# A four-layer attention and expert kernel: the shared expert's down products one step behind, its logits leaving per batch

## The reference

```python
logits = x @ w_router.T
_, top_idx = jax.lax.top_k(logits, TOP_K)
mask = jax.nn.one_hot(top_idx, E, dtype=logits.dtype).sum(axis=1)
scores = jax.nn.sigmoid(logits) * mask
...
shared = jax.nn.silu(x @ w_gate.T) * (x @ w_up.T) @ w_down.T
out = shared + expert_out.sum(axis=0)
...
x = x + _L0_xattn_ref(ctx_1024, _layernorm(x, axis=-1), ...)
x = x + _L0_ffn_ref(_layernorm(x, axis=-1), L0_ffn_w_router, ...)
x = x + _L1_xattn_ref(_layernorm(x, axis=-1), ctx_1024, ...)
x = x + _L1_ffn_ref(_layernorm(x, axis=-1), L1_ffn_gate_w, ...)
```

## Time and profile before

| what | value |
|---|---|
| time, median of 3 runs | 1640.59 us (1637.47 to 1646.26) |
| the profiled execution, its own time | 1626.23 us |
| its span, first to last instruction | 1624.5 us |
| PE busy | 1455.4 us (90%) |
| DVE, ACT, POOL busy | 942.9, 872.7, 638.1 us |
| mean granted clock of PE | 0.954 |

### The profile page before, as it was taken

One profiled execution on the slowest core, in us unless ns is written; L12 is line 12 of the kernel. 1 busy time (PEld: TensorE's weight loads), 2 busy tenths in 40 slices (PEclk: granted clock), 3 DMA queues, 4 the chain that ended last, 5 costly groups with the idle time before them and its releaser, 6 DMA issues. The chain is left out here.

```text
span 1624.5 us, 28386 instructions
## 1 busy us (share of the span) xinstructions
PE 1455.4 (90%) x9884; PEld 1191.8 (73%) x9884; DVE 942.9 (58%) x1771; ACT 872.7 (54%) x2184; POOL 638.1 (39%) x886
## 2 busy tenths in 40 slices
PE   4999999999999999888899994799998539999995
PEld 3878887878787888577888883566564528888885
DVE  5776767676767676655211116577787554444442
ACT  3886868677878686634111123566664214454442
POOL 6514444434444440322300015332321035777764
PEclk9999999999999999979999996999999559999998
DMA  4400000000000000012789853000000413455442
GB/s 135 167 1 21 1 21 2 21 3 20 2 20 2 1 2 1 1 34 72 267 310 316 306 192 48 26 8 14 8 1 1 136 52 116 118 127 119 119 124 27
DMA packets 74448, 120.27 MB, mean 74 GB/s; under 512 B 7008, under 2 KB 55136, under 8 KB 74304
## 3 DMA queue, kind: packets, MB, share of 16 engines
q1 hardware_dynamic: 63600, 101.76, 19.3%
q0 software_dynamic: 10704, 16.65, 5.1%
HBM read 99.78 MB, written 18.61 MB: 73 GB/s over the span
## 5 line engine op out<-in xcount | busy, mean ns | idle before, releaser
L508 ACT ACTIVATE a_p<-a_s,a_negmax 128x512 f32<-128x512 f32 x256 | 176.1, 688 | 111.4 <-DVE a_negmax L632 61.4
L632 DVE TENSOR_REDUCE a_negmax<-a_s 128x1 f32<-128x512 f32 x256 | 176.3, 689 | 74.3 <-PE a_s L371 68.0
L273 POOL TENSOR_TENSOR a_o_l<-a_o,a_o_h 128x256 fp32r<-128x256 f32 x64 | 46.9, 734 | 297.7 <-ACT a_o_h L533 297.7
L1546 ACT ACTIVATE h_probs<-h_scores,h_negmax 128x256 f32<-128x256 f32 x256 | 117.8, 473 | 82.0 <-DVE h_negmax L1713 82.0
L380 PEld LDWEIGHTS a_t<-ident,a_p 128*128 128x128 f32 x1024 | 122.3, 140 | 51.3 <-issue 22.8
L380 PE MATMUL a_t<-ident,a_p 128*128 128x128 f32 x1024 | 156.7, 276 | 0.7 <-DVE a_pT L647 0.7
L1958 POOL TENSOR_TENSOR n_w_l<-n_raw,n_w_h 128x768 fp32r<-128x768 f32 x64 | 118.1, 1847 | 74.6 <-ACT n_w_h L2001 74.6
L398 PE MATMUL a_out_p<-a_pT,a_v 128*64 128x256 f32 x1024 | 124.6, 385 | 0.0
L370 PE MATMUL a_s<-a_k_hl,a_q_hh 128*128 128x512 f32 x256 | 106.2, 415 | 2.2 <-issue 1.5
L1713 DVE TENSOR_REDUCE h_negmax<-h_scores 128x4 f32<-128x1024 f32 x64 | 78.0, 1219 | 49.5 <-PE h_scores L1640 49.5
L1651 PEld LDWEIGHTS h_turned<-ident,h_probs 128*128 128x128 f32 x512 | 55.1, 142 | 64.6 <-issue 45.8
(11 more groups left out here) (358 smaller groups left out, 4376.3 us busy)
## 6 DMA issues: line engine op xcount, KB each, us to landing
e_w_in<-in_L_ffn_gate_up_proj SPq DMA_DIRECT2D x31, 1024.0 KB, 7.1
n_raw<-in_L_ffn_w SPq DMA_DIRECT2D x64, 384.0 KB, 3.1
e_w_out<-in_L_ffn_down_proj SPq DMA_DIRECT2D x31, 512.0 KB, 5.3
rows_in<-a_zeros SPq DMA_DIRECT2D x1, 3968.0 KB, 15.8
e_rows<-rows_in SPq DMA_DIRECT2D x31, 128.0 KB, 5.1
rows_out<-e_result POOLq DMA_DIRECT2D x31, 128.0 KB, 4.8
a_both<-in_ctx SPq DMA_DIRECT2D x8, 256.0 KB, 2.8
a_both<-in_x SPq DMA_DIRECT2D x8, 256.0 KB, 3.0
```

Of the source, the lines that this page charges most:

```text
L508: act.activation(probs[j][:, :], scores[j % 2][:, :], ACT.Exp, bias=negmax[:, j:j + 1], accum_out=total[:, r % 2, j % 2, j // 2:j // 2 + 1 ...
L632: dve.tensor_reduce(negmax[:, j:j + 1], scores[j % 2][:, :], AX.X, ALU.max, negate=True).then_inc(max_set, 1)
L1546: ins = act.activation(probs[s % 4][:, j, :], scores[s % 2][:, j // 2, j % 2, :], ACT.Exp, bias=negmax[:, s % 4, j:j + 1], accum_out=total ...
```

## The change

What it does, with "unit" as above:

- `down` takes one chunk: `down(n)`, 12 matmuls, stands in PE's stream behind gate and up of unit n + 1. The four chunks of a group add up in PSUM, so the first of them waits for `add` of the group before (`added`). `s_hid_h` and `s_hid_l` are two buffers of one chunk each in place of one of four.
- The logits of a batch go to the bank of `small` that its transposes came through. DVE's new `take_logits(b)` sums their two halves into `r_logits` (64 elements in, 32 out, per partition). `turn_x(b)` now waits for `take_logits` of batch b - 2, not only for `xT_l`. In a unit, `find_logits(2n)` stands ahead of gate, and `find_logits(2n + 1)` between gate and up.
- route(0) stands inside unit 3 ahead of `s_hidden`, route(1) after unit 3, route(2) and route(3) after unit 4, route(4) after unit 5; `count` after unit 3 on PE. Two copies of route(0) go. `add(grp)` follows the units 4, 8 and the last early one.

```diff
-        hid_h, hid_l = sb("s_hid_h", [P, FC, N], F32R), sb("s_hid_l", [P, FC, N], F32R)
+        hid_h, hid_l = [sb(f"s_hid_h{i}", [P, N], F32R) for i in range(2)], [sb(f"s_hid_l{i}", [P, N], F32R) for i in range(2)]
...
-        logit_ps = sum_ps[1][:, :, :].rearrange("p i (t h e) -> p (i t) h e", h=2, e=E)
-        logits = within
+
+        logit_ps = [w[:, 0, 0:4 * E].rearrange("p (t h e) -> p t h e", h=2, e=E) for w in small]
+        logits = sb("r_logits", [P, NT, E])
...
-                def down(grp):
-                    pe.wait_ge(low, FC * (grp + 1))
-
-                    wait(pe, added, grp)
-                    passes = [(h, w, c) for c in range(FC)
-                              for h, w in ((hid_h, sw_h), (hid_h, sw_l), (hid_l, sw_h))]
+                def down(n):
+                    m, grp = n % FC, n // FC
+                    pe.wait_ge(low, n + 1)
+                    if m == 0:
+
+                        wait(pe, added, grp)
+                    if n == 0:
+                        pe.wait_ge(sl_set, 4)
                     for t in range(TILES):
-                        for k, (h, w, c) in enumerate(passes):
-                            ins = pe.matmul(sum_ps[t // 2][:, t % 2, :], h[:, c, t * P:(t + 1) * P], w[2][:, c, :],
-                                            start=(k == 0), stop=(k == len(passes) - 1))
-                    ins.then_inc(summed, 1)
+                        passes = ((hid_h, sw_h), (hid_h, sw_l), (hid_l, sw_h))
+                        for k, (h, w) in enumerate(passes):
+
+                            ins = pe.matmul(sum_ps[t // 2][:, t % 2, :], h[n % 2][:, t * P:(t + 1) * P], w[2][:, m, :],
+                                            start=(m == 0 and k == 0 and t % 2 == 0),
+                                            stop=(m == FC - 1 and k == len(passes) - 1 and t % 2 == 1))
+                    ins.then_inc(downed, 1)
...
-                    wait(pe, x_low, b - 1)
+                    wait(pe, logits_set, b - 1)
...
                 def find_logits(b):
                     pe.wait_ge(x_low, b + 1)
-                    for t in range(2 * b, 2 * b + 2):
-                        at = slice(t * P, (t + 1) * P)
+                    if b == 0:
+                        pe.wait_ge(rl_set, 1)
+                    for t in range(2):
+                        at = slice((2 * b + t) * P, (2 * b + t + 1) * P)
                         for kc in range(KC):
-                            pe.matmul(logit_ps[:, t, :, :], g.xT_h[:, kc, at], router_hl[:, kc, :, :], start=(kc == 0), stop=False)
-                            ins = pe.matmul(logit_ps[:, t, 0, :], g.xT_l[:, kc, at], router_hl[:, kc, 0, :], start=False, stop=(kc == KC - 1))
-                    if b == NB - 1:
-                        ins.then_inc(logits_done, 1)
+                            pe.matmul(logit_ps[b % 2][:, t, :, :], g.xT_h[:, kc, at], router_hl[:, kc, :, :], start=(kc == 0), stop=False)
+                            ins = pe.matmul(logit_ps[b % 2][:, t, 0, :], g.xT_l[:, kc, at], router_hl[:, kc, 0, :], start=False, stop=(kc == KC - 1))
+                    ins.then_inc(logits_done, 1)
 
                 def shared(n, first):
 
                     wait(pe, hidden_set, n - 1)
+                    if n < NB // 2:
+                        find_logits(2 * n)
                     if n % FC == 0 and n // FC * 2 < NB:
                         pe.wait_ge(x_low, 2 * (n // FC) + 2)
                     if n == 0:
                         pe.wait_ge(sl_set, 1)
                     product(gate_ps[n % 2], 0, n, gated)
                     if n < NB // 2:
-                        if n == 0:
-                            pe.wait_ge(rl_set, 1)
-                        find_logits(2 * n)
                         if 2 * n + 2 < NB:
                             turn_x(2 * n + 2)
+                        find_logits(2 * n + 1)
                     if n == 0:
                         pe.wait_ge(sl_set, 2)
                     product(up_ps[n % 2], 1, n, upped)
-                    if n < NB // 2:
-                        find_logits(2 * n + 1)
-                        if 2 * n + 3 < NB:
-                            turn_x(2 * n + 3)
-                    if n % FC == 0 and n > first:
-                        if n == FC:
-                            pe.wait_ge(sl_set, 4)
-
-                            pe.wait_ge(hot_set, 1)
-                        down(n // FC - 1)
+                    if 2 * n + 3 < NB:
+                        turn_x(2 * n + 3)
+                    if n > first:
+                        down(n - 1)
...
                     shared(n, 0)
-                    if n == FC:
+                    if n == FC - 1:
                         count()
-                down(EARLY - 1)
+                down(FC * EARLY - 1)
...
-                    down(GROUPS - 1)
+                    down(FC * GROUPS - 1)
...
-                    wait(act, summed, n // FC)
-                    act.activation(hid_h[:, n % FC, :], hidden[n % 2][:, :], ACT.Copy).then_inc(high, 1)
+                    wait(act, downed, n - 1)
+                    act.activation(hid_h[n % 2][:, :], hidden[n % 2][:, :], ACT.Copy).then_inc(high, 1)
...
-                        dve.wait_ge(logits_done, 1)
-                        link(dve.tensor_copy(logits[:, :, :], logit_ps[:, :, 1, :]))
-                        link(dve.tensor_tensor(logits[:, :, :], logit_ps[:, :, 0, :], logits[:, :, :], ALU.add))
+                        dve.wait_ge(logits_set, NB)
...
+                def take_logits(b):
+                    dve.wait_ge(logits_done, b + 1)
+                    dve.tensor_reduce(logits[:, 2 * b:2 * b + 2, :], logit_ps[b % 2].rearrange("p t h e -> p t e h"),
+                                      AX.X, ALU.add).then_inc(logits_set, 1)
...
                 def shared(n):
-                    if 2 * n + 2 < NB:
-                        take_low(2 * n + 2)
+                    if n < NB // 2:
+                        take_logits(2 * n)
+                        if 2 * n + 2 < NB:
+                            take_low(2 * n + 2)
+                        take_logits(2 * n + 1)
                         if 2 * n + 4 < NB:
                             apply(2 * n + 4)
+                    if n == NB // 2 - 1:
+                        route(0)
...
-                    dve.wait_ge(summed, grp + 1)
+                    dve.wait_ge(downed, FC * (grp + 1))
...
-                    if n in range(3, 8):
-                        route(n - 3)
+                    if n == 3:
+                        route(1)
+                    elif n == 4:
+                        route(2)
+                        route(3)
+                    elif n == 5:
+                        route(4)
                     elif n == 8:
                         scale_queries()
-                    if n % FC == 1 and n > FC:
+                    if n % FC == 0 and n:
                         add(n // FC - 1)
...
-                    if n % FC == 1 and n > FC * (EARLY + 1):
+                    if n % FC == 0 and n > FC * EARLY:
```

More of the change, by code:

```diff
@@ L863, in run_mixture @@
         gated, upped, silu_set, hidden_set = sem("s_gated"), sem("s_upped"), sem("s_silu_set"), sem("s_hidden_set")
-        high, low, summed, added = sem("s_high"), sem("s_low"), sem("s_summed"), sem("s_added")
+        high, low, downed, added = sem("s_high"), sem("s_low"), sem("s_downed"), sem("s_added")
         rows_in = [sem(f"e_rows_in{i}") for i in range(AHEAD)]
@@ L1308, in shared @@
                     dve.wait_ge(high, n + 1)
-                    dve.tensor_tensor(hid_l[:, n % FC, :], hidden[n % 2][:, :], hid_h[:, n % FC, :],
+                    dve.tensor_tensor(hid_l[n % 2][:, :], hidden[n % 2][:, :], hid_h[n % 2][:, :],
                                       ALU.subtract).then_inc(low, 1)
```

2 lines of the change are left out of this document (1 added, 1 removed).

## The result

The kernel after takes 1634.56 us (median of 20 runs, 1627.1 to 1640.98), the kernel before beside it 1639.72 us (20 runs, 1636.44 to 1646.26). The ratio is 0.9961, 95% interval 0.9947 to 0.9974: some 6.4 us faster, where the forecast was 0.6 us slower and no measurable change.

What follows compares the result with a forecast made beforehand. The prediction took PE, busy 90% of the span, as the bound, so its waits decide. Terms of -2.2, +1.6 and +1.2 us gave +0.6 us, 1641.2 us on the runs' median, range 1632 to 1649 us.

Steps and rivals of the forecast that it cites:

- the sum's last line: Whole kernel: +0.6 us on the profiled 1626.23 us, carried to the runs' median 1640.59 us, giving 1641.2 us.
- Start and units 1 to 2: Layer's start: new PE waits for take_logits, 1.7 us before turn_x(2) and 1.1 us in unit 1.
- The wait at down(4): Fifth chunk of down: PE waits 5.9 us for add(0), then one low-clock stretch costing 1.6 us.
- down(11): Last chunk before the experts: PE waits 1.0 us in place of 2.38 us.
- The early part in all: Layer's start to the experts: -2.2 us of waits and +1.6 us of clock, -0.6 us together.
- The tail: Units 12 to 15 to the layer's end: +1.2 us on DVE's chain, bounds 0 and +2.8 us.
- Clock stays low: Rival, units 1 to 3: new waits keep the clock at 0.50, some +18 us, 1659 us; chance 0.06.
- The scatters: POOL's 16 scatters before the experts: 6.8 us earlier, done near 772, ACT's weighing ahead of POOL, no gain or cost.
- Rows set the experts' start: Rival, experts' start: rows end last if PE's waits turn out small, -6.9 us, 1634 us; chance 0.08.

Runs made afterwards that it cites:

- after_third: The changed kernel, unchanged, timed beside the kernel before on a chip without the stalls: 1627.67 us, ratio 0.9991.
- after_again: The changed kernel, unchanged, timed and traced once more: 1636.43 us, ratio to the kernel before 0.9976.
- before_third: The kernel before, unchanged, traced a third time, on a chip without the stalls: 1628.54 us, ratio 0.9996.
- after_late_w: The changed kernel with the loads of the first three experts' weights all held until hidden_set 12: 1635.62 us, ratio to the kernel before 0.9975.
- old_routing: The changed kernel with the routing steps and the count back at their old places: 1630.89 us, ratio to the kernel before 0.9951.
- old_routing2: The changed kernel with routing steps and count at their old places, run again on a chip without the stalls: 1629.28 us, ratio to the kernel before 1.0.
- before_again: The kernel before, unchanged, profiled once more: 1640.51 us, ratio 1.0013.
- before_late_w: The kernel before with the loads of the first three experts' weights all held until hidden_set 12: 1637.28 us, ratio 0.9978.

## Why the prediction was wrong

**The step that failed** stands in the sum's last line: "the median of the runs, 1640.59, lies 14.4 us over that execution; the same 0.6 us on it give 1641.2". The 14.4 us were taken for a constant that lies on both kernels alike. They are not. By the later trace, 11.0 of them lie in the one stretch that the change reorders: stalls of ACT and DVE between 762 and 785 us, which the trace of the prediction does not have. The runs of before beside the result were not traced; their time, and the stall in the trace of after, say that they had them. The new order meets them with less harm. In before they end in front of gate(11) and down(2), where PE has nothing else to do: 11.0 us. In after one of them falls beside units 7 and 8, PE has up(7), down(6), gate(8) and up(8) to go on with, and 2.85 us of wait and 1.7 us of low clock are left of it, 4.6 us. 11.0 - 4.6 = 6.4 us. What is left of the early stretch is 86.4 - 4.6 = 81.8 us against 82.8, -1.0, and the tail gives +0.3 to +0.5: in all some 7 us, against 6.4 by the ratio and 5.2 by the medians. That the sum comes so close is in part luck: it rests on one trace of each kernel, and the ratio in the other sets with the stalls was 0.9976, 4 us.

Point by point:

- *Start and units 1 to 2*: 1.7 and 1.1 us forecast, 1.30 and 1.00 measured (the second is 0.20 in after_third and missing in after_again, where the clock is low there). take_logits takes 0.22 us, forecast 0.25. Unit 1 started at 718.63, forecast 717.9 with the layer 2.6 us earlier, so 1.8 us ahead of it, because the clock had risen at 714.5. The 8.0 and 6.9 us of units 1 and 2 add up to 14.9 and not to 14.8.
- *The wait at down(4)*: 5.9 us forecast, 5.54; row_of at 751.25, forecast 750.5 with the layer starting 2.6 us earlier than it did, so it too came 1.8 us ahead. The stretch at clock 0.50 came, but longer: 6.15 us, so +3.1 and not +1.6.
- *down(11)*: 1.0 forecast, 0.86.
- *The early part in all*: forecast -0.6 us. In one set without the stalls it was 83.5 against 83.7 us, -0.3. The start's clock alone moves a trace by more than that (below).
- *The tail*: the +1.2 us at normalise(1) came, but at the next layer's first matmul some 0.5 were left (53.5 us from unit 12 in after_third, 53.0 in before_third).
- *Clock stays low*: in part. The prediction called 0.50 beyond 720 us a sign that it is wrong. The result's own trace is at 0.50 only until 714.5. But of the eleven traces with the new start, four are low longer: after_third, after_late_w and old_routing until 721 to 722, after_again once more from 716 to 723. In the other seven 0.50 ends some 12 us after the first apply, in before's nine at 15 to 16 us (one: 20). So the new start gains some 2 us on before's or loses as much, never the 18 us of the rival.
- *The scatters*: forecast done near 772 with ACT's weighing ahead of POOL. In after POOL waits 4.12 us for it ahead of the thirteenth, in the stall of ACT, and starts the last at 774.83; in after_third it waits for nothing and starts the last at 772.18. PE waits for no rows in either.
- *Rows set the experts' start*: not in after, but in old_routing2, at 5.3 us.

So where the stalls are absent the forecast is not contradicted: +0.2 us by the terms measured (-0.3 + 0.5), a ratio of 0.9991 (0.9969 to 1.0012) measured. For the runs that count the forecast was wrong by 7 us, and a profiled execution faster than every run was the warning, which I read as a plain offset.

**What stays open** is what makes ACT and DVE stand still. Shown: it comes with the chip or its surroundings, not with the kernel (before's median was 1637 to 1640 us in four sets of runs and 1628 to 1629 us in four others, with nothing between; one chip number, 2, turned up in both groups, so it may be the machine or the hour); in before_again and before_late_w it returns at the same instructions to 0.04 us, while in the traces of after it keeps its length on DVE (6.86 and 6.96 us of idle before s_hidden(7) in after and after_again) but not on ACT (silu(7) starts at 767.49 in one and at 764.69 in the other); it isn't the weights' transfer. It isn't of ACT and DVE alone: in old_routing PE too stops four times between 776 and 781 us without a releaser, 2.0 us in all. Not shown: that the scatters, or the fetch of instructions, cause it. In the stretch from 745 to 792 us the packets of the two instruction queues took at most 1.32 us each with the stalls and 1.27 us without, and the scatters' packets 0.118 us on average in before_again and 0.116 in before_third, so neither transfer is itself the long one. Removing the scatters where the stalls are would tell, and all six runs of that kind met sets without them. For the 2.82 us of s_hid_l there is a better account (below), but it wasn't tested where it happens, either. And that the overlap of the stalls makes the gain rests on the accounts of PE's time in the traces and on the gain's absence where they are absent, not on a run that adds them.

## What to carry to other kernels

Before a sum is made on a trace, hold the trace's own time against the timed runs: where it lies outside their range, the missing microseconds sit somewhere, and they fall on the change or beside it. An idle time of an engine whose named releaser ended long ago, or that is put down to nothing, is a stall to be located first. In this kernel, work cut into small pieces that one engine can take between two others' results lost less to such stalls than one large piece at the end, even where the sum of ordinary waits said it gains nothing. And where a change has two parts, time each alone: here the second part, the earlier routing, brought nothing that the runs show.

## What the runs showed of the hardware

- The same kernel takes 1628 us in some sets of runs and 1637 to 1640 us in others, with 10 to 11 us of it inside one stretch of 30 us; the rest of the layer agrees (before: 181.9 to 183.5 us for the experts, 53 for units 12 to 15 in both).
- A DVE subtraction of 128x512 took 2.82 us in before_again (778.74 to 781.56) in place of 0.69, and 2.83 in before_late_w. In before_again POOL's two subtractions of the same shape run from 778.47 to 781.00, 1.27 us each, so DVE's ends when theirs are over and its own 0.6 us are done (timeline of before_again, POOL):

```profile
778.47 2.53 POOL L944 TENSOR_TENSOR w_l<-spare,w_h 128x512 fp32r<-128x512 f32 x2
```

  The Trainium skill (SBUF — State Buffer, section "SBUF: two separate sides") has DVE and GpSimd share one pair of ports by an exclusive lock, which an instruction holds to its end, also where a DVE instruction with two inputs in SBUF meets a GpSimd one that reads SBUF. The row agrees with that rule, save that by it DVE is held from its start until the first of the two ends at 779.7, and it waits out the second as well. It takes a late s_hid_l to meet POOL there: in the traces without the stalls DVE was through before POOL began.
- Waits of one length do not always have the same clock behind them: behind the wait of 2.9 us before gate(8) the granted clock read 1.00 for the next 5 us in the trace of the prediction and in before_again, and 0.50 for the next 5.61 us in before_third.
